# Orders around bank B, the last half tile and W's first cast in a per-sample low-rank recommender layer

## The reference, cut to what matters

```python
# x [2048, 1024] f32, user and item indices [2048] i32, W [1024, 1024], A [16, 1024]
# B_user, B_item [1250, 1024, 16], W_common [1024, 16]
base = x @ W_base.T + b_base
a = x @ A.T                                    # [2048, 16]
user_part = einsum('bor,br->bo', B_user[user_indices], a)
item_part = einsum('bor,br->bo', B_item[item_indices], a)
common_part = a @ W_common.T
return base + 2.0 * (user_part + item_part + common_part)
```

## Time and profile before

| | |
|---|---|
| median of 3 runs | 222.88 us (222.84 to 223.06) |
| profiled execution | 223.5 us, its span 221.7 us |
| TensorE busy (PE) | 213.9 us, 96% |
| VectorE busy (DVE) | 169.1 us, 76% |
| ScalarE, POOL busy | 55.3 us, 70.0 us |
| DMA | 57.76 MB, mean 261 GB/s |

### The profile page before, as it was taken

One profiled execution on the slowest core, in us unless ns is written; L12 is line 12 of the kernel. 1 busy time (PEld: TensorE's weight loads), 2 busy tenths in 40 slices (PEclk: granted clock), 3 DMA queues, 4 the chain that ended last, 5 costly groups with the idle time before them and its releaser, 6 DMA issues.

```text
span 221.7 us, 3023 instructions
## 1 busy us (share of the span) xinstructions
PE 213.9 (96%) x1122; PEld 172.8 (78%) x1122; DVE 169.1 (76%) x261; ACT 55.3 (25%) x87; POOL 70.0 (32%) x81
## 2 busy tenths in 40 slices
PE   7999999799999997999999999999999999989995
PEld 7777887587777875877887788878887888868894
DVE  1889988899499799999999999399997982070411
ACT  3686526434011120034100223045010600000000
POOL 6010250040324422415643263114544240573000
PEclk9999999999999999999999999999999999999999
DMA  6999999755739975798899999866899948158121
GB/s 203 394 415 370 268 338 412 259 206 233 228 94 312 385 279 234 218 286 330 318 282 308 362 281 313 312 256 235 296 333 367 356 174 190 42 171 159 56 100 49
DMA packets 14816, 57.76 MB, mean 261 GB/s; under 512 B 3828, under 2 KB 4468, under 8 KB 10812
## 3 DMA queue, kind: packets, MB, share of 16 engines
q0 software_dynamic: 7344, 35.30, 47.5%
q1 hardware_dynamic: 7168, 21.73, 27.6%
q10 hardware_dynamic: 288, 0.52, 0.7%
HBM read 58.95 MB, written 11.01 MB: 316 GB/s over the span
## 4 chain that ended last, share of the span: by engine, by line
PE 50%; DVE 21%; DMA 18%; SPq 5%; issue 3%; ACT 2%; DVEq 0%; POOLq 0%
PE main_ps L1012 14%; PE main_ps L1014 14%; PE main_ps L1013 14%; DVE acc L731 11%; DMA rows<-table,fetch 7%; DMA out_sb<-table 6%; DVE x_lo L634 4%; DMA set_sums<-acc 2%; PE main_ps L1078 2%; SPq L295 2%; DMA x_hi_raw<-set_sums,back 2%; DVE a_turned L684 2%; SPq L298 1%; PE ps_b L968 1%; PE ps_b L969 1%
## 5 line engine op out<-in xcount | busy, mean ns | idle before, releaser
L731 DVE SCALAR_TENSOR_TENSOR acc<-rows,a_entry,acc 128x1024 f32<-128x1024 f32 x75 | 96.3, 1284 | 8.6 <-DMA rows<-table,fetch 6.5
L1012 PE MATMUL main_ps<-w_hi,x_hi 128*128 128x512 f32 (+1 forms) x224 | 87.9, 392 | 0.0
L1014 PE MATMUL main_ps<-w_hi,x_lo 128*128 128x512 f32 (+1 forms) x224 | 86.5, 386 | 0.0
L1013 PE MATMUL main_ps<-w_lo,x_hi 128*128 128x512 f32 (+1 forms) x224 | 86.5, 386 | 0.0
L399 POOL DMA_INDIRECT rows<-table,fetch x40 | 50.4, 1261 | 105.5 <-DVE acc L731 92.9
L1014 PEld LDWEIGHTS main_ps<-w_hi,x_lo 128*128 128x128 f32 x224 | 42.1, 188 | 8.7
L1012 PEld LDWEIGHTS main_ps<-w_hi,x_hi 128*128 128x128 f32 x224 | 42.1, 188 | 7.9
L1013 PEld LDWEIGHTS main_ps<-w_lo,x_hi 128*128 128x128 f32 x224 | 42.2, 188 | 7.8
L634 DVE TENSOR_TENSOR x_lo<-x_lo_raw,x_hi 128x1024 fp32r<-128x1024 f32 (+2 forms) x19 | 19.9, 1054 | 1.3 <-ACT x_hi L483 1.0
L523 ACT ACTIVATE out_sb<-main_ps 128x1024 f32<-128x1024 f32 x12 | 12.2, 1018 | 31.8 <-PE main_ps L1014 30.5
L483 ACT ACTIVATE x_hi<-x_lo_raw 128x1024 fp32r<-128x1024 f32 (+2 forms) x18 | 16.8, 946 | 10.7 <-DMA x_lo_raw<-x_t 10.7
(11 more groups left out here) (116 smaller groups left out, 158.6 us busy)
## 6 DMA issues: line engine op xcount, KB each, us to landing
out<-out_sb SPq DMA_DIRECT2D x15, 512.0 KB, 6.0
x_lo_raw<-x_t SPq DMA_DIRECT2D x14, 512.0 KB, 8.2
w_lo_raw<-w_t SPq DMA_DIRECT2D x7, 512.0 KB, 7.2
x_lo_raw<-x_t SPq DMA_DIRECT2D x3, 256.0 KB, 5.5
rows<-table,fetch POOLq DMA_INDIRECT x40, 8.1
w_lo_raw<-w_t ACTq DMA_DIRECT2D x2, 256.0 KB, 4.2
set_sums<-acc SPq DMA_DIRECT2D x1, 512.0 KB, 5.1
out_sb<-table SPq DMA_DIRECT2D x6, 64.0 KB, 12.4
```

Of the source, the lines that this page charges most:

```text
L731: return dve.scalar_tensor_tensor(to, rows_r, a_r, to, ALU.mult, ALU.add)
L1012: pe.matmul(to, x_hi[:, u % RING, k, x], w_hi[:, k, o], start=start, stop=False)
L1013: pe.matmul(to, x_hi[:, u % RING, k, x], w_lo[:, k, o], start=False, stop=False)
L1014: return pe.matmul(to, x_lo[:, u % RING, k, x], w_hi[:, k, o], start=False, stop=stop)
```

## The change

- TensorE, tile 15: the last half of the output is one sum of 512 columns in its own bank of `main_ps` (before: two of 256 columns, the second in bank A). VectorE evicts it with one instruction. SP stores its first 256 columns and ScalarE's queue its last 256.
- W's slice 0, first half: ScalarE casts columns 0 to 255, VectorE columns 256 to 511, right behind its cast of x's first piece. TensorE's first product waits for both.
- VectorE: `turn_a_values(2)` comes before `make_x_lo(3, 0)`, `spread_values(2)` and `take_rows(1)` between the two pieces of `x_lo` of unit 3; `make_x_lo(5, 1)` comes right behind `make_x_lo(5, 0)`; `take_entries(2)` comes before the last chunk of set 1's products.
- TensorE: `pack_entries(1)` comes ahead of `turn_low(3)`, two slices of `base(3, ...)` earlier.
- POOL: `add_to_out(2)` comes behind `bring_back()`.

```diff
-def parts_of(n):
-    last = n == TILES - 1
-    return ((0, BANK), (BANK, 3 * BANK // 2), (3 * BANK // 2, OUT_F)) if last else ((0, BANK), (BANK, OUT_F))
+def half_of(part):
+    return slice(part * BANK, (part + 1) * BANK)
+QUARTER = BANK // 2
...
-        stores = [16 * (TILES // 2), 16 * (TILES // 2 + len(parts_of(TILES - 1)) - 1)]
-        def sums_of(n, part):
-            if len(parts_of(n)) > HALVES and part == HALVES:
-                return ps_a[:, 0:BANK // 2]
-            c0, c1 = parts_of(n)[part]
-            return main_ps[n % MAINS][:, c0:c1]
+        stores = [16 * (TILES // 2), 16 * (TILES // 2 + 2)]
...
             t = TILES - 1
-            for part, (c0, c1) in enumerate(parts_of(t)):
-                o = slice(c0, c1)
+            for part, o in enumerate((half_of(0), slice(BANK, BANK + QUARTER))):
                 sp.wait_ge(evacuated, t + 1 + part)
                 sp.dma_start(out[t * P:(t + 1) * P, o], out_sb[:, t % 2, o]).then_inc(stored[t % 2], 16)
...
             gather(4, range(0, CHUNKS))
+            bring_back()
             add_to_out(2)
-            bring_back()
             add_to_out(3)
...
-            make_first_w_hi(0, w_half_loaded)
-            make_first_w_hi(1, w_loaded[0])
+            make_first_w_hi(slice(0, QUARTER), w_half_loaded)
+            make_first_w_hi(half_of(1), w_loaded[0])
...
             clear_done_x(3)
+            t, o = TILES - 1, slice(BANK + QUARTER, OUT_F)
+            act.wait_ge(evacuated, t + HALVES)
+            act.dma_start(out[t * P:(t + 1) * P, o], out_sb[:, t % 2, o]).then_inc(stored[t % 2], 16)
...
             dve.tensor_copy(x_piece(x_hi, 0, 0), x_piece(x_raw, 0, 0)).then_inc(x_first_hi, 1)
+            dve.wait_ge(w_half_loaded, 16)
+            dve.tensor_copy(w_hi[:, 0, QUARTER:BANK], w_raw[:, 0, QUARTER:BANK]).then_inc(w_first_hi, 1)
             make_x_lo(0, 0)
+            dve.wait_ge(w_first_hi, 1)
             make_w_lo(0)
...
             spread_values(1)
+            turn_a_values(2)
             make_x_lo(3, 0)
+            spread_values(2)
+            take_rows(1)
             make_x_lo(3, 1)
-            take_a(2)
-            take_rows(1)
             take_entries(0)
...
             make_x_lo(5, 0)
-            row_products(1, range(2, 3))
             make_x_lo(5, 1)
-            row_products(1, range(3, 5))
+            row_products(1, range(2, 5))
             make_onehot(3)
             take_a(5)
-            row_products(1, range(5, CHUNKS))
+            row_products(1, range(5, 7))
             take_entries(2)
+            row_products(1, range(7, CHUNKS))
...
-            for part, (c0, c1) in enumerate(parts_of(TILES - 1)):
-                evacuate_with_sums(TILES - 1, sums_of(TILES - 1, part), slice(c0, c1), TILES - 1 + part)
+            t = TILES - 1
+            for part in range(HALVES):
+                evacuate_with_sums(t, main_ps[t % MAINS][:, half_of(part)], half_of(part), t + part)
...
+                    if k == 0 and half == 0:
+                        pe.wait_ge(w_first_hi, 1)
...
             base(3, range(0, 2))
+            pack_entries(1)
             turn_low(3)
-            base(3, range(2, 4))
-            pack_entries(1)
-            base(3, range(4, KC)).then_inc(tile_done, 1)
+            base(3, range(2, KC)).then_inc(tile_done, 1)
```

More of the change, by code:

```diff
@@ L228, in rec_kernel @@
         w_loaded = [sem(f"w_loaded{k}") for k in range(KC)]
-        w_half_loaded, x_first_hi = sem("w_half_loaded"), sem("x_first_hi")
+        w_half_loaded, x_first_hi, w_first_hi = sem("w_half_loaded"), sem("x_first_hi"), sem("w_first_hi")
         last_loaded, left_loaded = sem("last_loaded"), sem("left_loaded")
@@ L483, in make_x_hi, with make_first_w_hi @@
                 act.activation(x_piece(x_hi, u, h), x_piece(x_raw, u, h), ACT.Copy).then_inc(x_hi_done, 1)
-            def make_first_w_hi(half, loaded):
-                o = slice(half * BANK, (half + 1) * BANK)
+            def make_first_w_hi(o, loaded):
                 act.wait_ge(loaded, 16)
@@ L1009, in base_step @@
                 u, j = divmod(t, UT)
-                x, o = slice(j * P, (j + 1) * P), slice(*parts_of(t)[part])
-                to = sums_of(t, part)
+                x, o = slice(j * P, (j + 1) * P), half_of(part)
+                to = main(t, part)
                 pe.matmul(to, x_hi[:, u % RING, k, x], w_hi[:, k, o], start=start, stop=False)
@@ L1014, in base_step, with base @@
                 return pe.matmul(to, x_lo[:, u % RING, k, x], w_hi[:, k, o], start=False, stop=stop)
-            def base(t, ks, start=False, parts=None, stop=True):
+            def base(t, ks, start=False, parts=range(HALVES), stop=True):
                 if 0 in ks:
@@ L1022, in base @@
                 for k in ks:
-                    for part in range(len(parts_of(t))) if parts is None else parts:
+                    for part in parts:
                         done = base_step(t, part, k, start and k == 0, stop and k == KC - 1)
@@ L1064, in left_of @@
                         pe.wait_ge(evacuated, UT * u + j - MAINS + 1)
-                if u == UNITS - 1:
-                    pe.wait_ge(bank_a_taken, len(TURNS_A))
                 for j in range(UT):
-                    for part, (c0, c1) in enumerate(parts_of(UT * u + j)):
-                        half = c0 // BANK
+                    for half in range(HALVES):
                         q = slice((j * HALVES + half) * LEFT, (j * HALVES + half + 1) * LEFT)
-                        pe.matmul(sums_of(UT * u + j, part), low_t[q, u % LOW_RING, UT * P:NLT],
-                                  left_w[q, c0 - half * BANK:c1 - half * BANK], start=starts[j], stop=stop)
+                        pe.matmul(main(UT * u + j, half), low_t[q, u % LOW_RING, UT * P:NLT], left_w[q, :],
+                                  start=starts[j], stop=stop)
             def last_of(t, stop=False):
                 u, j = divmod(t, UT)
-                for part, (c0, c1) in enumerate(parts_of(t)):
-                    done = pe.matmul(sums_of(t, part), low_t[:, u % LOW_RING, j * P:(j + 1) * P],
-                                     last_w[:, c0:c1], start=False, stop=stop)
+                for part in range(HALVES):
+                    done = pe.matmul(main(t, part), low_t[:, u % LOW_RING, j * P:(j + 1) * P],
+                                     last_w[:, half_of(part)], start=False, stop=stop)
                 return done
@@ L1168, in _ @@
                     base(t0, range(1, KC)).then_inc(tile_done, 1)
-                    for part in range(len(parts_of(t1))):
+                    for part in range(HALVES):
                         base(t1, range(0, KC), parts=range(part, part + 1)).then_inc(tile_done, 1)
```

## The result

The changed kernel takes 219.69 us, median of 4 runs (219.28 to 220.49), against 222.89 us before (222.84 to 223.06, 4 runs). The ratio is 0.985, interval 0.9814 to 0.9886. The forecast was 218.6, range 218.0 to 220.4: the direction and the range held, the gain came out at 3.2 us instead of 4.3. The profiled execution is the slowest of the four, 220.49, span 218.8. Nine of the runs told further down had a granted clock of 0.990 to 0.992, all others 0.996 or more: one each of a7 and a10, which are left out of their medians and ranges, and seven of the kernel before, each at 224.87 us or more, which stand in its medians and in the ratios (four of them in those of a1 to a4).

A forecast was written before the change was run, and what follows sets the result against it. TensorE, busy 96% of the span, was taken as the bound, with five idle places totalling 4.44 us. Removing them, with +0.1 for the last stores, gave -4.3: 222.88 to 218.6 us, range 218.0 to 220.4.

The forecast's parts named there:

- Four stalls of TensorE: Idle before pack_rows(1), turn_low(4), rank_a(5) and pack_rows(3) goes: 1.58, 0.25, 1.72 and 0.30 us.
- the one at 82 us: TensorE's 0.25 us idle before turn_low(4), waiting for VectorE's low, was to go.
- W's first cast: Sharing the cast of W's first slice at the start is worth 0; bounds -0.2 and +0.3 us.
- VectorE's lead: VectorE runs 3.85 us ahead at take_entries(1), 3.7 carried on; row products end at about 180.4.
- The gather waits I leave as they are: VectorE's gather waits, 6.5 us over the kernel, stay: gathers and loads move by 1.8 to 3.9, meeting as before.
- The gate: TensorE's 0.59 us wait before left_of(7) for tile 12's eviction, behind row products, store and gathers, goes; margin 1.4.
- rival A: Gather chain decides: VectorE gains under 3.7 or set_sums stays at 5.1, TensorE waits before left_of(7); 219.7 to 221; chance 0.22.
- both shortfalls: VectorE 2.5 us short of its 3.7 and the set_sums store still at 5.1: 221.
- add_to_out(2): Issued behind bring_back, it leaves the set_sums store alone: landing 3.2 us instead of 5.1; later adds stay covered by 6.
- Last half tile: At the end, one 512-column sum equals two of 256 up to the last eviction: 6.39 against 6.37 us.
- The pair of stores: Two last 128 KB stores issued at once land within bounds 1.7 and 2.0 us; taken as +0.1.
- the forecast's own sum: Over the whole kernel, -4.44 + 0.1, so -4.3 us, taken from the median of 222.88: 218.6.

The follow-up runs named there:

- a7: Changed kernel with the old tail: last half tile as two sums of 256 columns, each evicted and stored by itself by SP; 219.66 us, ratio 0.9847.
- a10: Changed kernel with add_to_out(2) ahead of bring_back again; 219.59 us, ratio 0.9835.
- a1: The changed kernel again, unaltered, on the chip of the variants beside it; 219.54 us, ratio 0.9796.
- a4: Changed kernel with the wait for tile 12 moved behind tile 14's base products and the last half tile as one 256 KB SP store; 219.87 us, ratio 0.9815.
- a11: Changed kernel with x_lo(5, 1) behind two row products again; 221.00 us, ratio 0.9888.
- a9: Changed kernel with pack_entries(1) back at its old place, two slices of base(3) behind turn_low(3); 220.85 us, ratio 0.9878.
- a8: Changed kernel with ScalarE casting all of the first half of W's first slice again; 219.43 us, ratio 0.9838.
- a12: Changed kernel, but SP stores tile 3 first and holds unit 5's loads of x until the seventh chunk is used; 219.98 us, ratio 0.9864.
- a3: Changed kernel with the last half tile stored by SP in one transfer of 256 KB; 219.27 us, ratio 0.9795.
- a5: Changed kernel with four slices of tile 14's base products ahead of the last unit's left_of and last_of, kept one group; 219.20 us, ratio 0.9821.
- a6: As a5, with the last half tile evicted in two instructions of 256 columns and stored by SP in two 128 KB transfers; 219.10 us, ratio 0.9818.

## Why the prediction was right in direction and 1.1 us short

- **Four stalls of TensorE: right.** Forecast 3.85, measured 4.17 (1.55, 0.36, 1.79, 0.47). a11 gives one back (1.6 of idle) and is 1.3 to 1.5 slower; a9 brings back the one at 82 us (0.40 from the end of the product ahead of it).
- **W's first cast: right as far as it can be seen.** a8 shows no difference. The 0.24 in the table is the landing of W's second half, whose cast starts at 5.54 here and at 5.86 in the earlier trace rows; a1 has it the other way round.
- **VectorE's lead: right at first, then the step that failed.** It was 4.2 us ahead at `take_entries(1)` (3.85 forecast), 4.7 at chunk 8 (69.30 against 73.96), 2.3 at chunk 9, and 0.7 when the row products ended (183.42 against 184.13; forecast 3.7). "The gather waits I leave as they are" was wrong. VectorE, whose progress times the gathers, moved by 4.2 and TensorE, whose progress times the loads of x, by 1.9. The loads for unit 5 went out 3.3 us ahead of the gather for chunk 9 (64.95 and 68.28) and now go out 1.0 ahead of it (63.06 and 64.05), and that gather lands in 10.4 instead of 8.5 us (timelines of SP and POOL of the changed kernel, landing of that gather). a12 moves the loads and gives back 1.2 of the 3.16. The rest of the lead went between 150 and 184 us, where chunks follow the gathers' landings. Why the row products end up to 3.8 us later in one execution than in another stays open. At `take_entries(4)` the executions already lie 2.6 apart (151.3 in a10 and a12, 153.1 in the changed kernel, 153.9 in a7), and the gathers' median landing is 9.0 us in the changed kernel, 8.1 in a10 and 8.4 in a12.

```profile
63.06 0.82 SPq L288 DMA_DIRECT2D x_lo_raw<-x_t  x2
```

```profile
64.05 1.39 POOL L391 DMA_INDIRECT rows<-table,fetch  x1 [2.44 <-DVE acc L725]
```

```profile
DMA to landing us min/median/max: 10.4/10.4/10.4
```

- **The gate: the mechanism was named, and rival A was what happened in part of the executions.** With the row products late, `set_sums` in 2.6 (3.2 forecast) doesn't save it. Seven profiled executions have this gate where the changed kernel has it, the same tail but for a3's single store, and no stall of 1.6 us on the way. In four of them the row products end at 183.4 to 183.8: TensorE waits 0.9 to 1.4, and the time is 220.5 to 221.2 (the changed kernel, a1, a8, a9). In the other three they end at 180.1 to 180.6: no wait or 0.1, and 219.0 to 219.3 (a3, a10, a12). That is why the changed kernel's runs spread over 1.2 us. a5 takes the gate away: slowest run 219.28, spread 0.21. It shows the gate, and the medians put its mean price at 0.3 to 0.5 (219.54 or 219.69 to 219.20), across groups. Rival A had VectorE 2.5 us short and 219.7. VectorE came out 3.0 short, `set_sums` landed faster and the tail was longer, so that the median is 219.69 is luck. (Its price with both shortfalls, given as 221, comes to 221.6 by its own figures: 2.5 + 1.9 - 1.4 = 3.0.)
- **add_to_out(2): the size was off.** The landing fell as forecast and more (by 2.5 us, 1.9 forecast), but a10 shows no measurable worth of the order in its median; the adds themselves ended far from the end, as forecast (last issue 203.55, landing 6.5).
- **Last half tile: mis-sized.** The equality up to the last eviction held within 0.04. The pair of stores was put at +0.1, bounds 1.7 and 2.0 to landing; ScalarE's took 2.5, and the tail grew by 0.7. By the rule of the Trainium skill cited in the forecast (DMA: Bandwidth & Descriptors, Issuing engines are not separate DMA queues) it would have been +0.3: nearer, and still low. That the pair behaves as one store of 256 KB is what a3 shows, within 0.1; it is the 2.0 for such a store that doesn't hold at the end of the kernel. Both bounds came from stores that were followed by work, or were half the size.

With the tail as measured, 0.6 above its term, the forecast's own sum gives 219.2, and a5, without the gate, has 219.20. That agreement is partly luck. In the same two traces the other terms gained 0.6 more than forecast (-0.24 at W's slice, -0.32 in the four stalls, -0.06 up to the last eviction), which takes the sum back to 218.6. The forecast subtracted losses read from an execution of 223.5 from a median 0.6 lower; no trace of a median execution of the kernel before shows which of its losses were smaller.

## What to carry to other kernels

Where two chains arrive within a microsecond of each other, forecast the margin with its run-to-run movement, not with one trace's value; then move the point where they meet, as a5 does: here that cost nothing measurable and took the spread from 1.2 to 0.2 us. When one engine's work is moved ahead more than another's, list which transfers now come closer together: here loads that had gone out 3.3 us ahead of a gather went out 1.0 ahead of it, and the gather landed 1.9 later after its issue. And price the last transfer of a kernel by one of its size in the same place.

## What was not expected of the hardware

- Of two 128 KB stores issued together at the end, the one from ScalarE's queue landed in 2.5 us and SP's in 1.9; alone, such a store took 1.7. One of 256 KB as the last transfer didn't make the span shorter by more than 0.1.
- Short last transfers (a6) made the profiled execution 0.4 faster and its span 0.7 shorter, the other executions 0.1 faster and their spans 0.3 shorter. Why the two differ wasn't found.
- The kernel before, with the same gate 0.6 late, was steady within 0.2 us in its first four runs. Its 26 later runs at a granted clock of 0.998 or more spread over 1.3 to 1.7 us in a group (223.04 to 224.37, 222.56 to 224.25, 222.53 to 224.21); why wasn't found.
